# Local attention scores held once per head, their softmax weights copied out over the head elements by transfers, and new orders for the first half

## The chip, the cores and the metric

The kernel runs on one NeuronCore of a Trainium2 chip. Its engines are TensorE (PE), VectorE (DVE), ScalarE (ACT), GpSimd (POOL) and SyncE (SP, which here only issues transfers). Each engine runs its own instructions strictly in order and waits on semaphores for the others. The metric is the device time of one launch in microseconds, median of the runs.

## What is computed

Two layers on x of 8 images of 512 tokens by 128 channels, all in 32-bit floats. Each layer is an attention part and a mixture of experts (8 experts, two per token).

The change lies in layer 0's attention part. A 64-wide projection of the layer-normalised x is split into two branches of 32 channels, with 8 heads of 4 elements each. Branch 0 uses windows of 10 tokens, branch 1 windows of 20, both rolled by half a window:

```python
attn = jnp.einsum('bnqhd,bnkhd->bnhqk', q * scale, k)
attn = attn + bias[None, None]
if amask is not None:
    attn = attn + amask[None, :, None]
attn = jax.nn.softmax(attn, axis=-1)
out = jnp.einsum('bnhqk,bnkhd->bnqhd', attn, v).reshape(Bx, nW, window, C)
```

So every image has 52 windows of 10 and 26 to 28 of 20 tokens, and one small softmax for each window, head and query. Behind it stand an output projection, a residual, an RMS norm and a feed-forward part (GELU), and beside it the experts (a gated unit of 128 units), which every token visits twice, and a shared expert. Layer 1 is a global attention over 512 tokens and another mixture of experts; the change leaves it alone.

## The kernel before, in words

**Stages.** All eight images are first normalised and projected down ("stats", "norm", "down", then "xi", about the first 83 us). Then comes a long software pipeline, layer 0. It ends at about 573 us; layer 1 follows and takes the rest.

**What is in the pipeline.** Two streams are interleaved. One is the chain of images: per image b the steps `("window", b, n)`, `("qk", b, n)`, the pieces "sub1" and "mul1", and `("tail", b, k)`. The other is 31 "passes" k (8 of the shared expert, 23 of blocks of 512 sorted token rows): "sorted" (the rows of the block turned on TensorE), "pair" (up-projections), "gate", "clip", "silu", "act", "down_e" and "yev". GpSimd also sends all token rows to their sorted places in DRAM ("send", 64 indirect transfers); pass 8 and later passes can only load their rows once all were sent.

**What sets the order.** `plan0(engine)` gives each step a due time in slots and sorts by it. An image begins every 9 slots, a pass every 3. The table `MOVED` shifts kinds of steps on one engine by fractions of a slot. So the tables decide the order on every engine, and nothing is reordered at run time.

**Attention of one image, before.** The partitions hold 4 groups of windows by 32 channels (8 heads by 4 elements). Per partition that is 13 windows of 10 by 10 and 7 of 20 by 20, 1300 + 2800 = 4100 elements.
- GpSimd forms q times k for every element (`products`, L1162) in 10 chunks, into `G`.
- TensorE multiplies with `HEADSUM` (L654), a block matrix of 4 by 4 ones: it sums the 4 elements of a head and writes the sum four times, once to each of its partitions. So scores stand four times in PSUM bank 4 or 5.
- VectorE adds bias (and mask) on the way to `WS` (L1430, 10 adds), takes row maxima into `WM` (L1402), subtracts them in branch 0 (L1438); GpSimd subtracts in branch 1 (L1170, 7 pieces). ScalarE takes exponentials of all 4100 elements. VectorE sums them (L1406) and takes reciprocals (L1408).
- The weights times v: branch 0 on VectorE (L1443), branch 1 on GpSimd (L1179, 7 pieces "mul1"). VectorE reduces over keys (L1414) and scales by the reciprocal (L1415) into `WO`, which TensorE projects (L666, L670) in tail step 0.

**Others that the prediction meets.** L1474 is a pass's gate product, L1481 and L1484 its clips. L1137 is a reciprocal root on GpSimd, L1220 the low part of a split of layer 1 weights, L1217 adds a bias. L440 is SyncE's one helper for all its transfers. `passing` loads a pass's weights and rows, `split` stores split weights, "yev" stores an expert block.

## Time and profile before

| | |
|---|---|
| Median of 3 runs | 1521.94 us (1521.86 to 1532.23) |
| Span of the profiled execution | 1519.2 us |
| PE, DVE, ACT, POOL busy | 1045.4, 1030.7, 663.6, 584.1 us |
| Mean granted TensorE clock | 0.840 |
| Until the pipeline's start, the pipeline, the rest | 82.8, 490, 946 us |

The page gives the profiled execution's span, from the first to the last instruction, and no other time for it; it is 2.7 us under the median. The shares of busy time are averages over stages with quite different limits, so the rows below are taken from single stretches.

### The profile page before, as it was taken

The page shows a single profiled execution, that of the slowest core. Times are in us where ns is not written, and L with a number is a line of the kernel's source. Part 1 is how long each engine was busy: PE and PEld are TensorE (multiplying, and loading weights), DVE is VectorE, ACT ScalarE, POOL GpSimd, SP SyncE. Part 2 cuts the span into 40 slices and gives each one's busy share as a digit, 9 for nine tenths or more (in the row PEclk, how much of TensorE's full clock was granted, in tenths as well). Part 3 has the DMA queues.
Part 4 walks back from the last instruction along what each step waited for, and adds up shares of the span by engine and source line. Part 5 has one row for each costly group of instructions (what it writes and reads, how often), then busy time and mean ns, then how long its engine had stood idle before and what let it go on. Part 6 is the DMA issues. An engine that isn't in the chain of part 4 may idle for free.

```text
span 1519.2 us, 16287 instructions
## 1 busy us (share of the span) xinstructions
PE 1045.4 (69%) x5366; PEld 569.4 (37%) x5366; DVE 1030.7 (68%) x1481; ACT 663.6 (44%) x909; POOL 584.1 (38%) x591
## 2 busy tenths in 40 slices
PE   4456365777787680263785757999977878787885
PEld 4423133444444340122232215888832323232331
DVE  3376366998899842378979635666667867686871
...
DMA packets 77948, 126.41 MB, mean 83 GB/s; under 512 B 16297, under 2 KB 35242, under 8 KB 77866
## 3 DMA queue, kind: packets, MB, share of 16 engines
...
q10 hardware_dynamic: 480, 0.79, 0.4%
...
## 4 chain that ended last, share of the span: by engine, by line
PE 33%; DVE 20%; POOL 16%; issue 10%; ACT 8%; DMA 8%; SPq 4%; ACTq 0%; POOLq 0%; DVEq 0%
PE PS L846 6%; PE PS L702 6%; DMA KS<-MAG 4%; POOL XS0D L1204 4%; POOL XS1D L1253 4%; PE PS L865 4%; SPq L440 4%; ACT P L913 4%; DVE MX L1647 3%; PE PS L604 3%; PE PS L609 2%; POOL WS L1179 2%; PE PS L769 2%; PE PS L805 2%; PE PS L823 2%
## 5 line engine op out<-in xcount | busy, mean ns | idle before, releaser
L1647 DVE TENSOR_REDUCE MX<-PS 128x2 f32<-128x1024 f32 x256 | 306.2, 1222 | 128.4 <-PE PS L785 122.6
L913 ACT ACTIVATE P<-PS 128x1024 f32<-128x1024 f32 x256 | 262.3, 1025 | 177.4 <-PE PS L823 174.0
L785 PE MATMUL PS<-KS,QS 62*128 62x512 f32 x512 | 141.9, 552 | 73.4 <-DVE MX L1647 47.6
L1235 POOL DMA_INDIRECT A<-Y1D,POS x64 | 74.3, 1161 | 266.8 <-DMA Y1D<-YE 184.8
L823 PE MATMUL PS<-QS,KS 64*128 64x512 f32 x512 | 125.4, 486 | 68.0 <-ACT P L913 56.6
L805 PE MATMUL PS<-P,V 128*32 128x512 f32 x1024 | 157.3, 691 | 0.1
L785 PEld LDWEIGHTS PS<-KS,QS 62*128 62x128 f32 x512 | 54.3, 209 | 218.5 <-DVE MX L1647 107.5
L702 PE MATMUL PS<-XST,WB 128*128 128x512 f32 x184 | 107.6, 718 | 11.0 <-issue 11.0
L654 PE MATMUL PS<-G,HEADSUM 128*128 128x400 f32 (+2 forms) x160 | 75.2, 592 | 55.4 <-POOL G L1162 44.7
L846 PE MATMUL PS<-XRH,WH 128*128 128x512 f32 (+1 forms) x276 | 104.2, 419 | 0.0
L1261 POOL TENSOR_TENSOR MAG<-MAG,EH 128x1024 f32<-128x1024 f32 x7 | 16.5, 2358 | 225.2 <-ACT MAG L913 225.1
L823 PEld LDWEIGHTS PS<-QS,KS 64*128 64x128 f32 x512 | 54.3, 207 | 117.3 <-ACT P L913 93.8
L1162 POOL TENSOR_TENSOR G<-QKV 128x400 f32<-128x400 f32 (+1 forms) x80 | 73.5, 919 | 37.5 <-ACT QKV L930 29.1
L1235 POOL DMA_INDIRECT YG<-Y0D,POS x64 | 64.7, 1011 | 48.3 <-DMA Y0D<-YE 29.2
L1253 POOL DMA_INDIRECT XS1D<-XN,POS x64 | 64.6, 1010 | 48.3 <-DVE POS L1377 29.1
L1204 POOL DMA_INDIRECT XS0D<-XN,POS x64 | 65.7, 1026 | 27.4 <-issue 23.6
L913 ACT ACTIVATE TH<-PS 128x512 f32<-128x512 f32 (+1 forms) x69 | 41.2, 598 | 76.1 <-PE PS L846 76.0
L865 PEld LDWEIGHTS PS<-W,A 128*128 128x128 f32 (+1 forms) x552 | 71.9, 191 | 6.5
L1170 POOL TENSOR_TENSOR WS<-WS,WM 128x400 f32<-128x400 f32 x56 | 57.8, 1032 | 41.5 <-DVE WM L1402 37.9
L865 PE MATMUL PS<-W,A 128*128 128x128 f32 (+1 forms) x552 | 72.4, 274 | 0.0
L1582 DVE SCALAR_TENSOR_TENSOR SL<-TH,PS 128x512 f32<-128x512 f32 (+1 forms) x69 | 47.2, 683 | 37.1 <-ACT TH L913 37.0
L1179 POOL TENSOR_TENSOR WS<-WS,QKV 128x400 f32<-128x400 f32 x56 | 61.4, 1096 | 20.8 <-DVE WM L1406 17.1
...
## 6 DMA issues: line engine op xcount, KB each, us to landing
...
```

The lines of the kernel that those rows point to most:

```text
L702: ins = pe.matmul(PS[:, 2 * pair + m, :], w[:, at:at + 128], x, start=True, stop=True)
L785: signal(pe.matmul(PS[:, s % 4, :], QS[rows, u % 3, hp, 128 * t:128 * t + 128], KS[rows, u % 3, hp, :], start=True, stop=True), "ms")
L805: ins = pe.matmul(PS[32 * a:32 * a + 32, 6, :], V[:, u // 2 % 2, k, at:at + 32], P[:, m % 2, a, :], start=k == 0, stop=k == NT - 1)
L823: signal(pe.matmul(PS[:, 4 + s % 2, :], KS[rows, u % 3, hp, 128 * k:128 * k + 128], QS[rows, u % 3, hp, :], start=True, stop=True), "st")
L846: ins = pe.matmul(out, WH[:, j % 2, w, f:f + m], x[:, j % 2, :], start=n == 0, stop=n == 2)
L865: ins = pe.matmul(PS[:, 4 + j % 2, 128 * t:128 * t + 128], A4[0:m, q % 3, 128 * t:128 * t + 128], W2[0:m, j % 2, c, :], start=c == 0 and t ...
L913: act.activation(*a, **k).then_inc(sem[name], 1)
L1179: go(f"wpv{r}", pool.tensor_tensor(t, t, bc(v, [128, hi - lo, k, k], 2), ALU.mult))
L1204: pool.indirect_dma_start(XS0D, bass.IndirectOffsetOnAxis(POS[0][:, k, g:g + 1], 0), XN[:, g, :], None).then_inc(sem["sent"], 16)
L1235: pool.indirect_dma_start(dst[:, k, t, :], None, src, bass.IndirectOffsetOnAxis(pos[:, k, g:g + 1], 0)).then_inc(sem[name], 16)
L1253: pool.indirect_dma_start(XS1D, bass.IndirectOffsetOnAxis(POS[1][:, k, g:g + 1], 0), XN[:, g, :], None).then_inc(sem["sent1"], 16)
L1647: go("mx", dve.tensor_reduce(MX[:, u % 2, t].rearrange("p (o h) -> p o h", o=2)[:, :, hp], PS[:, s % 4 - 1:s % 4 + 1, :], AX.X, ALU.max))
```

## The change

**Scores once per head.** `HEADSUM` becomes 128 by 32 with ones for the 4 elements of each head. One matmul gives 32 rows of scores (4 groups of windows by 8 heads) for 400 columns, and four (or three) of them, with different columns of `G`, fill the four blocks of 32 partitions of one PSUM bank. All scores of an image are then 3 groups of 400 per partition, 1200 elements instead of 4100, in the new tile `WD`: groups 0 and 1 are branch 1 (4 and 3 windows), group 2 is branch 0.

**Then, on 1200 elements:** 3 adds of bias and mask on VectorE, 2 maxima, the subtraction of both branches on GpSimd ("less", 2 instructions), one exponential, 2 sums and one reciprocal of 80 on VectorE, and a new multiplication of weights by reciprocal on GpSimd ("even", 2 instructions).

**Weights copied out.** `spread` on SyncE's queue copies them from `WD` to `WS`: 11 transfers an image, each reading 32 partitions four times and writing 128 partitions, 1600 or 1200 bytes to each, in all 2.10 MB (7 of them, 1.43 MB, for branch 1, then 4, 0.67 MB, for branch 0). The products with v are all on GpSimd (branch 0 in 2 pieces, "mul0"), and VectorE's reduction over keys gives `WO` directly. `WS` is single now, `QKV` triple, `G` four rows of 400.

**Orders.** The window steps run over 21 slots instead of 19, the `MOVED` table is new, and SyncE has shifts of its own. TensorE turns a block's rows 3 slots earlier. Before the pipeline, GpSimd builds the bias tables before it waits for the sums of squares, not after; the masks come from DRAM.

```diff
-PIECES = {"sub1": ONES_OF, "mul1": ONES_OF}
...
+GROUPS = 3
+QK_AT = {5: 0, 7: 1, 9: 2}
+PIECES = {"mul0": [(0, 6), (6, 13)], "mul1": [(w, w + 1) for w in range(NWIN[1])]}
+PIECE_AT = {"mul0": 17, "mul1": 17.5}
...
-CHUNK_AT = {5: (0, 2), 6: (2, 4), 7: (4, 6), 8: (6, 8), 9: (8, 10)}
-WEXP_AT = (12, 13)
-FRONT = 19
+LESS_AT, EXP_AT, SUM_AT, EVEN_AT, SPREAD_AT, OUT_AT = 11.5, 12, 13, 13.5, 14, 20
+FRONT = 21
+CELL = WIN[1] ** 2
+TURN0 = 3
...
+MOVED = {'POOL': {('window', 11): 0.1, 'send': -0.9, ('tail', 2): 1.0, ('qk', 6): -0.6, 'sub1': -1, ('qk', 5): -1, 'split': 2.9, 'mul0': 0.6, ('qk', 2): 1.9, ('less', 0): 1.0, 'mul1': -1.1, ('tail', 3): 0.1, ('less', 1): -0.6}, 'DVE': {('tail', 1): 0.7, 'yev': 1.4, ('window', 14): -1.5, ('qk', 9): 1.5, ('window', 18): 0.1, ('qk', 6): 0.4, ('window', 11): 1.0, ('qk', 8): 0.1, ('qk', 7): 0.3, ('window', 20): -0.6, 'clip': 0.1, 'act': 0.4, ('window', 13): 0.6, ('tail', 3): 0.6, ('window', 10): 0.1, ('window', 7): -0.3}, 'PE': {'down_e': 1.7, ('tail', 6): -1, ('window', 10): 1.7, ('tail', 7): -0.8, ('window', 8): 0.8, ('window', 6): 0.7, 'sorted': -3.0, ('tail', 1): -0.6, ('tail', 0): -0.7, ('window', 3): -0.1, ('tail', 4): 0.5, ('pair', 1): 1, ('window', 4): -0.1}, 'ACT': {('tail', 6): -1, ('tail', 2): -0.6, ('window', 3): 0.8, 'split': 1.8, ('tail', 0): -0.7, 'sorted': -2.6, ('window', 4): 0.1, ('window', 12): 0.1, 'silu': 1, ('gate', 0): -0.1}, 'plan': {'period': 9, 'step': 3, 'start': 1}, 'SP': {('window', 14): 2.4, ('pair', 0): 1.9, 'yev': 5.8, 'split': 5.8}}
...
+        for r in (1, 0):
+            put(period * b + LESS_AT, ("less", b, r))
+            put(period * b + EVEN_AT, ("even", b, r))
...
+            QKV = [sb0(f"QKV{r}", [128, 3, 3, GRP[r]]) for r in range(2)]
+            G = sb0("G", [128, 4, CELL])
+            WD = sb0("WD", [128, 2, GROUPS, CELL])
+            WM = sb0("WM", [128, 2, 40])
+            WS = sb0("WS", [128, S_W])
...
+        def window_rows(r, b):
+            return (WD[:, b % 2, 0:2] if r else WD[:, b % 2, 2:3]).rearrange("p c (n k) -> p (c n) k", k=WIN[r])
...
+            def spread(b):
+
+                sp.wait_ge(sem["weven"], 2 * b + 2)
+                for r in (1, 0):
+                    if b:
+                        sp.wait_ge(sem[f"wout{r}"], b)
+                    wide = WS[:, S_AT[r]:S_AT[r] + GRP[r] * WIN[r]].rearrange("p (w a) -> p w a", a=WIN[r] ** 2)
+                    for s in range(4):
+                        rows = slice(32 * s, 32 * s + 32)
+                        if r:
+                            for p in range(2 if s < 3 else 1):
+                                load(wide[:, 4 * p + s], bc(WD[rows, b % 2, p], [32, 4, CELL], 1), "wide1")
+                        else:
+                            n = TURN0 + (s == 3)
+                            src = WD[rows, b % 2, 2, 0:n * WIN[0] ** 2]
+                            dst = wide[:, TURN0 * s:TURN0 * s + n].rearrange("p w a -> p (w a)")
+                            load(dst, bc(src, [32, 4, n * WIN[0] ** 2], 1), "wide0")
+
             for what, *a in plan0("SP"):
...
+                if n - 1 in QK_AT:
+                    c = QK_AT[n - 1]
+                    pe.wait_ge(sem["prod"], GROUPS * b + c + 1)
+                    if c == 2:
+                        pe.wait_ge(sem["S_sb"], GROUPS * b + 1)
+                    else:
+                        pe.wait_ge(sem["qkv_sb"], 2 * b + 2)
+                    flat = G[:].rearrange("p s a -> p (s a)")
+                    for s in range(4 - (c == 1)):
+                        at = TURN0 * WIN[0] ** 2 * s if c == 2 else CELL * s
+                        ins = pe.matmul(PS[32 * s:32 * s + 32, 4 + c % 2, 0:CELL], HEADSUM[:], flat[:, at:at + CELL],
+                                        start=True, stop=True)
+                    signal(ins, "S")
 
...
-                if n in WEXP_AT:
-                    r = WEXP_AT.index(n)
-                    act.wait_ge(sem[f"wsub{r}"], len(PIECES.get(f"sub{r}", "1")) * (b + 1))
-                    s = WS[:, b % 2, S_AT[r]:S_AT[r] + GRP[r] * WIN[r]]
-                    go(f"wexp{r}", s, s, ACT.Exp)
+                if n == EXP_AT:
+                    act.wait_ge(sem["wsub"], 2 * b + 2)
+                    go("wexp", WD[:, b % 2], WD[:, b % 2], ACT.Exp)
...
+            def less_max(r, b):
 
                 pool.wait_ge(sem[f"wmax{r}"], b + 1)
-                k = WIN[r]
-                at = slice(*(x * k for x in piece))
...
+                t = window_rows(r, b)
+                go("wsub", pool.tensor_tensor(t, t, bc(WM[:, r], [128, 40, WIN[r]], 2), ALU.subtract))
+
+            def even(r, b):
+
+                pool.wait_ge(sem["wsum"], b + 1)
+                t = window_rows(r, b)
+                go("weven", pool.tensor_tensor(t, t, bc(WM[:, r], [128, 40, WIN[r]], 2), ALU.mult))
...
-                pool.wait_ge(sem[f"wexp{r}"], b + 1)
-                pool.wait_ge(sem[f"wsum{r}"], b + 1)
+                pool.wait_ge(sem[f"wide{r}"], 16 * (4, 7)[r] * (b + 1))
...
                 elif what == "xi":
-                    pool.wait_ge(sem["xi_sq"], 1)
-                    rsqrt(RSTDX[:], SQX[:], 1.0 / 64, 1e-6, "rstd_xi")
-                    pool.wait_ge(sem["w_b"], 16 * 18)
...
+                    pool.wait_ge(sem["xi_sq"], 1)
+                    rsqrt(RSTDX[:], SQX[:], 1.0 / 64, 1e-6, "rstd_xi")
...
-            def window_sum(b, r):
-                dve.wait_ge(sem[f"wexp{r}"], b + 1)
-                go(f"wsum{r}", dve.tensor_reduce(WM[r][:], window_scores(b, r), AX.X, ALU.add))
-                dve.wait_ge(sem[f"wsum{r}"], b + 1)
-                step(dve.reciprocal(WM[r][:], WM[r][:]))
+                dve.wait_ge(sem["S_sb"], GROUPS * b + (3, 2)[r])
+                if b:
+                    dve.wait_ge(sem["weven"], 2 * b)
+                go(f"wmax{r}", dve.tensor_reduce(WM[:, r], window_rows(r, b), AX.X, ALU.max))
+
+            def window_sum(b):
+                dve.wait_ge(sem["wexp"], b + 1)
+                for r in range(2):
+                    ins = dve.tensor_reduce(WM[:, r], window_rows(r, b), AX.X, ALU.add)
+                step(ins)
+                go("wsum", dve.reciprocal(WM[:], WM[:]))
...
-                step(dve.tensor_reduce(WO[r][:], window_scores(b, r), AX.X, ALU.add))
-                go(f"wout{r}", dve.tensor_tensor(WO[r][:], WO[r][:], WM[r][:], ALU.mult))
+                wide = WS[:, S_AT[r]:S_AT[r] + GRP[r] * WIN[r]].rearrange("p (n k) -> p n k", k=WIN[r])
+                go(f"wout{r}", dve.tensor_reduce(WO[r][:], wide, AX.X, ALU.add))
...
+                if n - 2 in QK_AT:
+                    c = QK_AT[n - 2]
+                    dve.wait_ge(sem["S"], GROUPS * b + c + 1)
+                    if c == 0 and b >= 2:
+                        for r in range(2):
+                            dve.wait_ge(sem[f"wout{r}"], b - 1)
+                    bias = LAST[0] if c == 2 else (BIAS, LAST)[c][1]
+                    flat = "p w q k -> p (w q k)" if c else "p q k -> p (q k)"
+                    rows = 96 if c == 1 else 128
+                    go("S_sb", dve.tensor_tensor(WD[0:rows, b % 2, c], PS[0:rows, 4 + c % 2, 0:CELL],
+                                                 bias[0:rows].rearrange(flat), ALU.add))
+                    dve.wait_ge(sem["S_sb"], GROUPS * b + c + 1)
...
-        "headsum": np.kron(np.eye(32, dtype=np.float32), np.ones((4, 4), np.float32)),
+        "headsum": np.kron(np.eye(32, dtype=np.float32), np.ones((4, 1), np.float32)),
```

Three places of the new orders. The first is GpSimd in the middle of the pipeline, from the last products of an image to the first of its products with v (`wide1` and `wide0` are the semaphores of the copies). Before:

```order
L1162 TENSOR_TENSOR G<-QKV 128x500 [waits S,prod] x2
L1162 TENSOR_TENSOR G<-QKV 128x300 [waits S,prod]
L1220 TENSOR_TENSOR SPL<-STAGE,SPH 128x704 [waits split_hi,prod]
L1170 TENSOR_TENSOR WS<-WS,WM 128x400 [waits wmax1,split_lo]
L1170 TENSOR_TENSOR WS<-WS,WM 128x400 [waits wmax1,wsub1] x6
L1136 TENSOR_SCALAR VAR<-SQ 128x4 [waits sqs0,wsub1]
L1137 TENSOR_TENSOR SCALES<-VAR,NHALF 128x4 [waits pstep]
L1162 TENSOR_TENSOR G<-QKV 128x400 [waits qkv_sb,rstd0]
...
L1217 TENSOR_TENSOR X<-X,FB 128x512 [waits h0,prod]
...
L1179 TENSOR_TENSOR WS<-WS,QKV 128x400 [waits wsum1,wexp1,prod]
L1179 TENSOR_TENSOR WS<-WS,QKV 128x400 [waits wsum1,wexp1,wpv1] x3
```

Now:

```order
L1185 TENSOR_TENSOR G<-QKV 128x700 [waits S,wpv1]
L1185 TENSOR_TENSOR G<-QKV 128x600
L1192 TENSOR_TENSOR WD<-WD,WM 128x800 [waits wmax1,prod]
L1248 TENSOR_TENSOR SPL<-STAGE,SPH 128x704 [waits split_hi,wsub]
L1192 TENSOR_TENSOR WD<-WD,WM 128x400 [waits wmax0,split_lo]
L1198 TENSOR_TENSOR WD<-WD,WM 128x800 [waits wsum,wsub]
L1198 TENSOR_TENSOR WD<-WD,WM 128x400 [waits wsum,weven]
L1185 TENSOR_TENSOR G<-QKV 128x400 [waits S,qkv_sb,weven]
...
L1164 TENSOR_SCALAR VAR<-SQ 128x4 [waits sqs0,prod]
...
L1185 TENSOR_TENSOR G<-QKV 128x400 x2
...
L1205 TENSOR_TENSOR WS<-WS,QKV 128x400 [waits wide1,x1_b]
L1205 TENSOR_TENSOR WS<-WS,QKV 128x400 [waits wide1,wpv1] x3
```

The seven subtractions became two, two multiplications (L1198) stand behind them, with nothing between the second subtraction and the first multiplication, which waits for the sums; and the products with v wait for transfers rather than for VectorE.

The second is VectorE about the softmax of an image; between the rows stand parts of the passes. Before, from the clips of a pass to the sum of branch 1:

```order
L1481 TENSOR_SCALAR UL<-UL 128x512 [waits gused]
L1484 TENSOR_SCALAR UL<-UL 128x512 [waits lused]
...
L1430 TENSOR_TENSOR WS<-PS,LAST 128x300 [waits S,S_sb]
L1402 TENSOR_REDUCE WM<-WS 128x130 [waits S_sb]
L1438 TENSOR_TENSOR WS<-WS,WM 128x1300 [waits wmax0]
...
L1406 TENSOR_REDUCE WM<-WS 128x130 [waits wexp0]
L1408 RECIPROCAL WM<-WM 128x130 [waits wsum0]
L1443 TENSOR_TENSOR WS<-WS,QKV 128x1300 [waits step]
L1414 TENSOR_REDUCE WO<-WS 128x130 [waits aux_full,wpv0]
...
L1406 TENSOR_REDUCE WM<-WS 128x140 [waits wexp1]
```

Now, from the last reduction of an image over keys (L1444) to the reciprocal of the next image (L1437):

```order
L1444 TENSOR_REDUCE WO<-WS 128x140 [waits wpv1]
L1484 TENSOR_TENSOR XN<-PS,X 128x512 [waits x1_b,aux_full]
L1494 SCALAR_TENSOR_TENSOR UL<-PS,WB,H 128x512 [waits aux_free,a,h3g,gpair]
...
L1504 TENSOR_SCALAR UL<-UL 128x512 [waits lused]
L1456 TENSOR_TENSOR WD<-PS,LAST 128x400 [waits S]
L1430 TENSOR_REDUCE WM<-WD 128x40 [waits weven,S_sb]
L1524 SCALAR_TENSOR_TENSOR YE<-B,PS 128x512 [waits sto1,y]
L1511 SCALAR_TENSOR_TENSOR AA<-UL 128x512 [waits y,lc,th]
L1435 TENSOR_REDUCE WM<-WD 128x40 [waits wexp]
...
L1437 RECIPROCAL WM<-WM 128x80 [waits step]
```

Rows with 1300 and 2800 inputs are gone save for L1444; the reduction of branch 1 of one image comes ahead of the last scores (L1456, L1430) of the next.

The third is SyncE, which now issues the copies (L447, WS<-WD) between a pass's loads and an expert block's store:

```order
L447 DMA STAGE<-in_w 128x352 x2
...
L447 DMA WB<-in_wb 128x644
...
L447 DMA XS<-XS0D 128x512 [waits aux_full]
L447 DMA WS<-WD 128x1x400 [waits wout1,weven]
L447 DMA WS<-WD 128x1x400 x6
L447 DMA WS<-WD 128x1x300 [waits wout0]
L447 DMA WS<-WD 128x1x300 x2
L447 DMA WS<-WD 128x1x400
L447 DMA Y0D<-YE 128x512 [waits yev]
L498 TENSOR_LOAD EB [waits yev]
```

Before, no such copies stood there; the store waited for `yev` right behind the loads, and the weight loads for `y` instead of `yev`.

## Rows read from the trace of the kernel before

**Rows 1.** The cores: span, and mean granted clock of TensorE.
```profile
core 0: 1519.2 us, clock 0.840
```

**Rows 2.** Three stretches: length, busy time (instructions) by engine, PEclk, DMA share, GB/s.
```profile
109.50:234.00 124.50, 61.77 (x252) 32.32 (x252) 66.47 (x76) 24.43 (x42) 103.48 (x103) 0.73 0.16 55
293.00:475.00 182.00, 141.03 (x736) 81.23 (x736) 164.05 (x174) 93.45 (x157) 118.59 (x113) 0.89 0.28 85
506.00:573.00 67.00, 50.89 (x204) 29.27 (x204) 41.21 (x55) 32.32 (x54) 13.97 (x14) 0.86 0.21 67
```

**Rows 3.** VectorE by line, 293 to 475 us: count, busy us, mean ns, idle before.
```profile
L1406 DVE TENSOR_REDUCE WM<-WS 128x140 f32<-128x2800 f32 (+1 forms) x9 | 21.3, 2365 | 0.0
...
L1430 DVE TENSOR_TENSOR WS<-PS,BIAS 128x400 f32<-128x400 f32 (+1 forms) x32 | 19.1, 596 | 3.8 <-PE PS L654 3.0
...
L1402 DVE TENSOR_REDUCE WM<-WS 128x140 f32<-128x2800 f32 (+1 forms) x8 | 18.3, 2288 | 0.3
...
L1414 DVE TENSOR_REDUCE WO<-WS 128x140 f32<-128x2800 f32 (+1 forms) x8 | 18.3, 2282 | 0.1
...
L1474 DVE SCALAR_TENSOR_TENSOR UL<-PS,WB,H 128x512 f32<-128x512 f32 x24 | 17.6, 748 | 10.9 <-ACT H L913 6.4 <-issue 4.3
...
L1484 DVE TENSOR_SCALAR UL<-UL 128x512 f32<-128x512 f32 x13 | 14.1, 1084 | 0.0
...
L1481 DVE TENSOR_SCALAR UL<-UL 128x512 f32<-128x512 f32 x12 | 10.3, 855 | 0.0
...
L1408 DVE RECIPROCAL WM<-WM 128x140 f32<-128x140 f32 (+1 forms) x8 | 8.0, 997 | 0.3
...
L1438 DVE TENSOR_TENSOR WS<-WS,WM 128x1300 f32<-128x1300 f32 x4 | 6.1, 1513 | 0.1
```

**Rows 4.** GpSimd by line, the same stretch.
```profile
L1162 POOL TENSOR_TENSOR G<-QKV 128x400 f32<-128x400 f32 (+2 forms) x41 | 37.7, 921 | 14.7 <-ACT QKV L930 10.3 <-PE PS L654 1.7
L1179 POOL TENSOR_TENSOR WS<-WS,QKV 128x400 f32<-128x400 f32 x28 | 31.0, 1106 | 10.6 <-DVE WM L1406 8.7
L1170 POOL TENSOR_TENSOR WS<-WS,WM 128x400 f32<-128x400 f32 x28 | 30.1, 1074 | 22.7 <-DVE WM L1402 20.8
L1137 POOL TENSOR_TENSOR SCALES<-VAR,NHALF 128x4 f32<-128x4 f32 x4 | 7.8, 1942 | 0.3
L1220 POOL TENSOR_TENSOR SPL<-STAGE,SPH 128x704 fp32r<-128x704 f32 x4 | 6.7, 1676 | 0.3
L1217 POOL TENSOR_TENSOR X<-X,FB 128x512 f32<-128x512 f32 x4 | 5.1, 1269 | 0.3
```

**Rows 5.** ScalarE by line, the same stretch: the exponential.
```profile
L913 ACT ACTIVATE WS<-WS 128x1300 f32<-128x1300 f32 (+1 forms) x8 | 15.3, 1910 | 13.0 <-DVE WS L1438 13.0
```

**Rows 6.** GpSimd by line, 109 to 235 us.
```profile
L1204 POOL DMA_INDIRECT XS0D<-XN,POS x64 | 65.7, 1026 | 27.4 <-issue 23.6 <-POOL WS L1170 1.4 <-POOL G L1162 1.4
```

**Rows 7.** Subtraction of the maxima by tile, whole run: count, ns min/median/max, first and last start.
```profile
L1170 POOL TENSOR_TENSOR WS<-WS,WM x56: 863/866/2217, 143.0 to 505.1; 128x400 f32<-128x400 f32 x56
```

**Rows 8.** TensorE in order of time: start us, us, line, count.
```profile
353.21 1.75 PE L654 MATMUL PS<-G,HEADSUM 128*128 128x400 f32 x4 [0.79 <-DVE WS L1430]
...
422.89 1.52 PE PS L641 x48
```

**Rows 9.** Stretches in which all DMA engines are busy, columns as in rows 2.
```profile
1404.00:1412.00 8.00, 7.08 (x52) 2.98 (x50) 5.77 (x5) 5.83 (x8) 2.65 (x3) 1.00 1.09 137
20.00:40.00 20.00, 12.57 (x59) 12.06 (x57) 6.77 (x34) 1.79 (x3) 2.49 (x4) 1.00 1.04 371
```

**Rows 10.** SyncE's issues of layer 1's copies inside SBUF: count, ns min/median/max.
```profile
L440 SPq DMA_DIRECT2D QS<-EH x64: 551/608/1235, 632.3 to 1430.9; - x64
```

**Rows 11.** Before the pipeline, in order of time: GpSimd, then VectorE.
```profile
74.22 3.50 POOL L1193 COPY BIAS<-RPB 128x10 f32<-128x10 f32 x10
...
81.63 1.03 POOL L1196 TENSOR_TENSOR LAST<-LAST,BIAS 128x400 f32<-128x400 f32 x1
...
82.69 0.42 DVE L1319 TENSOR_REDUCE RS<-PS 128x32 f32<-128x256 f32 x1 [6.21 <-POOL LAST L1196]
```

153 lines of the change are left out of this document (57 added, 96 removed), and 2 rows, old and new, of the table SIGNALS.

## The prediction, made before the changed kernel had run

> **What bounds the kernel now.** The core's row [rows 1] gives one span, 1519.2 us, 2.7 us under the median of the runs, so every sum below is made against 1519.2 and 2.7 is added at its end. I then read busy time by stretch [rows 2], because the change touches the first 573 us alone.
>
> From 109.5 to 234 us GpSimd is the bound: 103.5 of 124.5 us busy, and the 64 sends alone are 65.7 us with 23.6 us of issue gaps between them [rows 6]. Busy and gaps together fill the stretch. From 234 to 506 us lie six image periods, 272 / 6 = 45.4 us each. In four of them (293 to 475 us, 182 / 4 = 45.5) VectorE is busy 164.05 us, 41.0 an image or 90%; GpSimd 118.6, 29.6 an image; TensorE 141 [rows 2]. GpSimd idles ahead of its subtractions because of VectorE's maxima (20.8 us) and ahead of its values products because of VectorE's sums (8.7) [rows 4], and ScalarE ahead of the exponentials likewise (13.0) [rows 5]. So VectorE sets the period. From 506 to 573 us no engine is full: the last image and the last passes follow each other.
>
> **Rates per element**, each from a row: VectorE's reduction 2288 / 2050 = 1.12 ns [rows 3]; on GpSimd q times k 921 / 410 = 2.25, weights times v 1106 / 400 = 2.77 [rows 4], subtraction at its median 866 / 400 = 2.17 [rows 7]; ScalarE's exponential 1910 / 2050 = 0.93 [rows 5].
>
> **VectorE, per image** [rows 3]. Bias adds: 10 inputs of some 0.58 (5.8 us) become 3 (1.7): -4.1. Maxima 4.6 to 1200 x 1.12 = 1.35: -3.2. Sums the same: -3.2. Reciprocals 2.0 to 0.6 (80 columns in place of 270): -1.4. L1438, branch 0's subtraction, 1.5, goes to GpSimd, and so does its equal, branch 0's product with v: -3.0. The reduction over keys (L1414) stays at 4.6; its scaling goes, at a price I leave out. Together about -15, leaving some 26 of 41. VectorE is no longer the bound.
>
> **TensorE, per image.** HEADSUM takes 10 matmuls of up to 128 x 500 now; four records, two to a matmul, last 1.75 us [rows 8], so 0.88 a matmul and some 9 us. If the four blocks of 32 columns run beside each other, it is three times 0.88 = 2.6 us. The trace has matmuls into four such blocks: 24 of them, of 130 or 140 columns, in 1.52 us [rows 8]. One after the other at the HEADSUM's rate they would be 24 x 0.88 x 135 / 400 = 7.1. So I take 2.6. Were it otherwise, 11 x 0.88 = 9.7: TensorE has 182 - 141 = 41 us idle in four images and bears a microsecond more; only the loop below would feel part of it.
>
> **GpSimd, per image.** Products 9.2 as before. Subtractions: 7 pieces, 7.5 us, become 1200 x 2.25 = 2.7. "Even" is new: 2.7. Values: 2800 + 1300 elements x 2.77 = 11.3 instead of 7.8. Reciprocal root, split, and bias (L1137, L1220, L1217) 1.9 + 1.7 + 1.3. Together 30.8, where it is 29.6 now. So no engine's busy time fills 45 us any more; what counts is the loop through the single `WS`: values products, reduction over keys, the next copies, the next values products.
>
> **The loop, from the end of an image's last product with v (t = 0)**, in the order the engines have. VectorE: reduction of 2800 elements 3.1; then a residual add 0.75 (priced as the gate product of the same size), two gate products 1.5, two clips 1.9 [rows 3], the last bias add 0.6, maximum of 400 elements 0.45, that is 8.3. GpSimd's subtraction of 400 elements: 9.2. ScalarE's exponential of 1200: 10.3. VectorE's sums and reciprocal, 1.35 + 0.6, and handovers: 12.6. GpSimd, with nothing to do from 9.2 to 12.6, then "even": 15.3. Now it forks.
> - GpSimd: the products of 2800 elements 6.3, reciprocal root 1.9, bias of x 1.3 and gaps: about 25.0.
> - Transfers: 1.43 MB for branch 1, then 0.67 MB for branch 0. The trace of before has no copy of this form. **Bounds:** the slowest stretch with all DMA engines full is of layer 1's copies inside SBUF, 137 GB/s; the fastest, a zero fill from SBUF, 371 [rows 9]. I take 137, since it is the one of copies from SBUF to SBUF. With an estimated 1.5 us for start and receipt: branch 1 lands at 15.3 + 1.5 + 10.5 = 27.3, branch 0 at 32.2. Issuing seven copies at 0.61 each [rows 10] is 4.3 and hidden.
>
> From 27.3 GpSimd makes branch 1's pieces, 7.8, with then branch 0's, 3.6 (landed at 32.2, so no more waiting): 38.7, and with 1.3 for handovers and gaps **40 us a period**. At 371 it would be 25.0 + 11.4 + 0.6 = 37, since then GpSimd is later than the transfers. A period of 45.4 again would need branch 0 to land at 45.4 - 1.3 - 3.6 = 40.5, that is 2.10 MB in 23.7 us, 89 GB/s.
>
> First what the rows show: 137 GB/s with the engines full. The Trainium skill, "SBUF — State Buffer", section "Door 1: The DMA port swizzle", speaks against the change: partitions 0 to 31 reach 8 of the 16 ports, half the rate, and 0 to 63 no more than these. Each copy reads 32 partitions. Half of the zero fill's 371 by that rule is 186, with which branch 1 lands at 24.5 and branch 0 at 28.1, so the period would be 37; half of 137 gives the slow rival below. The copies of layer 1 read 64 partitions each, and by that page have their halving behind them; no run here shows which.
>
> **What else the change adds to.** SyncE waits for "even" in the middle of its queue; behind the wait stand the store of an expert block (its tile is double, so a pass of some 13 us covers it) and the next pass's weights. Other traffic is 85 GB/s over the period [rows 2], 3.9 MB an image, 1.3 MB a pass; I have it beside the copies at no cost, see the third rival. ScalarE loses 2 x 1.9 - 1.1 = 2.7 us an image of exponentials, worth nothing by itself.
>
> **The sum.**
> - Start: VectorE waited 6.21 us for `LAST`, since the tables (first copy at 74.22) stood on GpSimd behind the reciprocal root [rows 11]. Now they are made before that wait: -6.2.
> - Sends, 109.5 to 234: still GpSimd. Counted in both orders, what stands between first and last send is 34 us in the new one and some 35 in the old one at the same rates: -2, ends 0 and -4.
> - Steady: 6 x (45.4 - 40) = -32.
> - 506 to 573: the last passes have VectorE for themselves sooner and their rows are turned earlier, but an image takes 21 slots instead of 19: -4, ends 0 and -10.
> Together -44.2: 1519.2 - 44.2 + 2.7 = **1477.7, say 1477 us**. Its own range 1462 to 1490. Chance 0.47.
>
> **Rivals.**
> - *Copies quick*: at 165 GB/s or more, GpSimd's own work is the later branch; period 37, -18: 1459. For it: 371 and the page's rule on the wider figure. 0.20.
> - *Copies behind a pass's loads*: SyncE issues the weights and rows of a pass right ahead of them. 1.3 MB at 371 GB/s is 3.5 us, all of it on the loop: period 43.5, +21: 1498. Against it: `weven` comes long after these issues as a rule. 0.22.
> - *VectorE's wait only changed place*: the work of the passes between the steps of the softmax (VectorE, in order, waits for ScalarE's gates 6.4 us in four images [rows 3]) draws the loop out to today's 45.4: -12: 1510. 0.07.
> - *Slower*: reading 32 partitions four times over halves 137 to 68 GB/s. Branch 0 lands at 15.3 + 1.5 + 30.9 = 47.7, its product, handovers and gaps make a period of 52.6, 6 x 7.2 = +43 against before, less the 12.2 of the other terms: 1553. It decides where the period passes 45.4 + 12.2 / 6 = 47.4, which is 82 GB/s. Against it: the copies that gave 137 write only 16 partitions each and so are narrower than these, which write all 128. 0.04.
>
> Under 1% (15 us) I can't tell from no change. Cases below 1506.7: the forecast, the first two rivals and a small part of the third: **0.90**; within 1%: 0.06; slower: 0.04. The range takes in the quick copies and those behind loads: **1450 to 1506**.
>
> **What would show it.** In the trace after: VectorE busy near 26 us an image; HEADSUM's four matmuls in 0.8 us; the wait ahead of GpSimd's first product with v named as the copies, and of 2 us; a gap of 3 us ahead of "even" named as VectorE's reciprocal; copies 9 to 11 us from the first issue to branch 1's landing; the pipeline's end at about 573 - 44 = 529 us. No wait for the copies, and GpSimd busy through, would be the first rival; a late wait on SyncE's queue or a landing 14 us after "even" the second. The prediction is wrong in its foundation if the period is set elsewhere than on GpSimd and the copies, for instance by TensorE (35 us an image busy now, about 30 then), which at a low granted clock (0.73 in the stage of the sends [rows 2]) would come close to 40.

## The result: 1471.9 us, 3.4% less

The median is 1471.93 us (1468.32 to 1473.38, 4 runs) against 1521.9 before; the ratio is 0.9656 with a 95% interval of 0.9625 to 0.9686. The prediction was 1477. In the profile the span is 1470.1 us against 1519.2 [rows 1], 49.1 less. The number is close, but the copies, on which I had built the 40 us period, did not set it.

Two marks cut layer 0 in both traces: the first and last send, and the first gather of expert rows (YG), which ends the pipeline. Rows by tile of the kernel before, with first and last start:

```profile
L1204 POOL DMA_INDIRECT XS0D<-XN,POS x64: 957/962/2165, 109.5 to 232.1; - x64
L1235 POOL DMA_INDIRECT YG<-Y0D,POS x64: 943/955/1742, 576.2 to 752.2; - x64
```

And of the changed kernel:

```profile
L1230 POOL DMA_INDIRECT XS0D<-XN,POS x64: 955/962/1300, 106.3 to 220.0; - x64
L1263 POOL DMA_INDIRECT YG<-Y0D,POS x64: 943/955/1745, 525.5 to 700.8; - x64
```

So 3.2 us are won by the first send, 8.9 between first and last send (122.6 to 113.7), 38.6 from there to the first gather (344.1 to 305.5), and 1.6 are lost behind (943.0 to 944.6). That is 49.1.

The same views as [rows 2] to [rows 4], over four periods of the changed kernel (from one image's first product with v to that of the fourth image after it) and over the sends; first the stretches:

```profile
289.20:442.40 153.20, 122.98 (x747) 71.51 (x744) 96.08 (x124) 82.67 (x153) 116.40 (x104) 0.87 0.58 156
106.30:221.00 114.70, 39.34 (x188) 20.23 (x186) 37.30 (x53) 20.30 (x31) 94.75 (x92) 0.65 0.23 67
```

VectorE is busy 24.0 us an image (41.0 before, 26 expected), TensorE 30.7, GpSimd 29.1 of some 38. GpSimd by line in the four periods:

```profile
L1205 POOL TENSOR_TENSOR WS<-WS,QKV 128x400 f32<-128x400 f32 (+2 forms) x36 | 43.2, 1200 | 3.0 <-DMA WS<-WD 0.2
L1185 POOL TENSOR_TENSOR G<-QKV 128x400 f32<-128x400 f32 (+2 forms) x36 | 37.1, 1059 | 8.9 <-PE PS L683 5.7 <-issue 1.8 <-POOL WD L1198 0.9
L1192 POOL TENSOR_TENSOR WD<-WD,WM 128x800 f32<-128x800 f32 (+1 forms) x8 | 9.7, 1209 | 9.2 <-DVE WM L1430 8.9
L1198 POOL TENSOR_TENSOR WD<-WD,WM 128x800 f32<-128x800 f32 (+1 forms) x8 | 9.7, 1209 | 14.6 <-DVE WM L1437 14.3
```

The right-hand numbers are the thing to read: they are GpSimd's idle time ahead of a line's instructions and what ended it. Ahead of the products with v (L1205) GpSimd waits 0.2 us in four images for the copies. Its idle time lies elsewhere: 3.6 us an image ahead of "even" for VectorE's reciprocal (3.4 expected), 2.2 for the maximum, 1.4 for TensorE's scores. One period in order of time:

```profile
327.82 11.48 POOL L1205 TENSOR_TENSOR WS<-WS,QKV 128x400 f32<-128x400 f32 x9
339.37 2.56 POOL L1185 TENSOR_TENSOR G<-QKV 128x700 f32<-128x700 f32 x2
342.01 1.54 POOL L1192 TENSOR_TENSOR WD<-WD,WM 128x800 f32<-128x800 f32 x1
343.63 1.68 POOL L1248 TENSOR_TENSOR SPL<-STAGE,SPH 128x704 fp32r<-128x704 f32 x1
347.85 0.87 POOL L1192 TENSOR_TENSOR WD<-WD,WM 128x400 f32<-128x400 f32 x1 [2.54 <-DVE WM L1430]
352.29 2.50 POOL L1198 TENSOR_TENSOR WD<-WD,WM 128x800 f32<-128x800 f32 x2 [3.56 <-DVE WM L1437]
```

SyncE issues the 11 copies right behind "even" of the image before, from 315.41 on (GpSimd had ended it at 315.39):

```profile
315.41 9.71 SPq L447 DMA_DIRECT2D WS<-WD  x11
```

That is 0.88 us an issue on average and 4.1 us (the median) from an issue to its landing, so branch 1 is complete 6 x 0.88 + 4.1 = 9.4 us after the first issue by these two; a wait in a later run (even_dve_qkv, below) gives 10.1. So it is there at some 325 to 325.5, and the product that needs it starts at 327.82: two microseconds or more to spare. The period, from the first products at 289.17 to those at 478.77, is 189.6 / 5 = 37.9 us.

The five periods are not alike. The first four, in the columns of [rows 2]:

```profile
289.17:327.82 38.65, 31.43 (x186) 18.46 (x186) 23.31 (x31) 20.39 (x38) 28.99 (x27) 0.82 0.63 168
327.82:365.61 37.79, 30.73 (x189) 17.77 (x189) 24.32 (x31) 20.58 (x39) 29.13 (x27) 0.86 0.53 147
365.61:405.77 40.16, 32.48 (x189) 18.95 (x189) 24.38 (x31) 20.93 (x39) 29.14 (x27) 0.83 0.63 169
405.77:442.44 36.67, 28.41 (x192) 16.33 (x189) 24.11 (x31) 20.84 (x40) 29.16 (x27) 0.95 0.51 137
```

GpSimd's work is the same in each, 29.0 to 29.2 us. The shortest period is the one with TensorE's highest granted clock, 0.95, the two longest those with 0.82 and 0.83 (1.00 is 2.4 GHz, and these are means of stretches at 2.4 and at 1.2). In the period of 40.16 GpSimd waits 2.53 us for TensorE's scores, in that of 36.67 not at all. So GpSimd's chain runs through TensorE too, and the period goes with its clock. Which of the two leads isn't shown, since no run changes the clock alone. The fifth period (36.33) has no next image's products to make, and 2.41 us of waiting for the copies.

### The profile page after: what moved, and what is told of

Same layout as the page of the kernel before. It is cut to its first block, busy times and chain, and to the rows that moved or that the text cites. A ratio compares the mean times of both kernels' runs of the same rounds, so it can differ in the third digit from the quotient of the medians.

```text
span 1470.1 us, 16140 instructions
## 1 busy us (share of the span) xinstructions
PE 1004.3 (68%) x5382; PEld 548.7 (37%) x5382; DVE 900.9 (61%) x1385; ACT 645.6 (44%) x902; POOL 578.9 (39%) x570
## 4 chain that ended last, share of the span: by engine, by line
PE 23%; DVE 11%; DMA 7%; ACT 7%; POOL 6%; issue 5%; SPq 4%; ACTq 0%; DVEq 0%; POOLq 0%
PE PS L876 6%; DMA KS<-MAG 4%; POOL XS1D L1281 4%; PE PS L895 4%; ACT P L943 4%; SPq L447 4%; DVE MX L1667 3%; PE PS L835 3%; PE PS L853 2%; PE PS L799 2%; PE PS L815 2%; ACT MAG L943 1%; PE PS L637 1%; DVE MAG L1596 1%; PE PS L632 1%
## 5 line engine op out<-in xcount | busy, mean ns | idle before, releaser
L815 PE MATMUL PS<-KS,QS 62*128 62x512 f32 x512 | 143.1, 557 | 70.1 <-DVE MX L1667 40.1
L732 PE MATMUL PS<-XST,WB 128*128 128x512 f32 x184 | 100.1, 686 | 0.0
L1185 POOL TENSOR_TENSOR G<-QKV 128x400 f32<-128x400 f32 (+2 forms) x72 | 73.5, 1048 | 41.0 <-ACT QKV L960 15.4
L1205 POOL TENSOR_TENSOR WS<-WS,QKV 128x400 f32<-128x400 f32 (+2 forms) x72 | 85.3, 1184 | 8.0 <-DMA WS<-WD 2.6
L1281 POOL DMA_INDIRECT XS1D<-XN,POS x64 | 64.0, 1000 | 48.3 <-DVE POS L1405 29.1
L1263 POOL DMA_INDIRECT YG<-Y0D,POS x64 | 64.3, 1005 | 37.6 <-DMA Y0D<-YE 18.5
L1230 POOL DMA_INDIRECT XS0D<-XN,POS x64 | 62.9, 983 | 24.7 <-issue 21.4
L1494 DVE SCALAR_TENSOR_TENSOR UL<-PS,WB,H 128x512 f32<-128x512 f32 x46 | 34.0, 748 | 57.0 <-ACT H L943 43.4
```

The costliest lines, as they stand in the source:

```text
L732: ins = pe.matmul(PS[:, 2 * pair + m, :], w[:, at:at + 128], x, start=True, stop=True)
L815: signal(pe.matmul(PS[:, s % 4, :], QS[rows, u % 3, hp, 128 * t:128 * t + 128], KS[rows, u % 3, hp, :], start=True, stop=True), "ms")
L1185: ins = pool.tensor_tensor(dst, bc(q[:, lo:hi], full, 3), bc(kk[:, lo:hi], full, 2), ALU.mult)
L1205: go(f"wpv{r}", pool.tensor_tensor(t, t, bc(v, [128, hi - lo, k, k], 2), ALU.mult))
L1263: pool.indirect_dma_start(dst[:, k, t, :], None, src, bass.IndirectOffsetOnAxis(pos[:, k, g:g + 1], 0)).then_inc(sem[name], 16)
L1281: pool.indirect_dma_start(XS1D, bass.IndirectOffsetOnAxis(POS[1][:, k, g:g + 1], 0), XN[:, g, :], None).then_inc(sem["sent1"], 16)
```

## Experiments

The kernels ran on three chips: start_back, the copies twice and few, and even_later on one, after_again, even_dve, even_dve_qkv and headsum_full on the second, the rest on the third. On the first and third the kernel before took 1592 and 1590 us, on the second 1522. The difference lies in layer 1: from the first gather to the end it is 1012.8 us in start_back and 944.6 in the changed kernel, while the first send of every kernel but start_back lies between 105 and 107 us. So each kernel is read by the start of its first gather, the end of layer 0's pipeline: 525.5 us in the changed kernel, 576.2 before. Ratios are to the kernel before on the same chip. On the first and third chip there is no trace of the changed kernel or of the one before; that layer 0 takes the same time there isn't shown directly. But what each run saves against the kernel before by full times on its own chip (57.0 us for copies_few, say) agrees within 5 us with what its first gather says (56.0), in every run.

### The start

GpSimd's tables again behind the sums of squares (start_back):

```diff
                 elif what == "xi":
+                    pool.wait_ge(sem["xi_sq"], 1)
+                    rsqrt(RSTDX[:], SQX[:], 1.0 / 64, 1e-6, "rstd_xi")
                     pool.wait_ge(sem["w_b"], 16 * 20)
...
-                    pool.wait_ge(sem["xi_sq"], 1)
-                    rsqrt(RSTDX[:], SQX[:], 1.0 / 64, 1e-6, "rstd_xi")
```

> The changed kernel with one thing undone: GpSimd again builds the bias tables behind its wait for the sums of squares and the reciprocal root. Theory: VectorE's routing reductions start at 82.7 us again instead of 77.1, the first send moves from 106.3 back to about 109.5, and the kernel takes 3 to 6 us more, 1475 to 1478. Rival: the sends start when the routing is done, which other work sets, and the start was worth nothing: 1472.

Ratio 0.9752 (0.9701 to 0.9803). VectorE's wait is back:

```profile
82.94 0.42 DVE L1347 TENSOR_REDUCE RS<-PS 128x32 f32<-128x256 f32 x1 [6.41 <-POOL LAST L1222]
```

The first send is at 110.8 (106.3), the first gather at 529.7: 4.2 us. VectorE's routing starts 5.8 us later than in the changed kernel (82.94 against 77.11), the first send only 4.5; what takes up the rest isn't shown. So a wait of 6.2 us was worth 4.2.

### The copies: twice, few, half

Seven more transfers an image, ahead of branch 1's, to a scratch area (copies_twice):

```diff
-                                load(wide[:, 4 * p + s], bc(WD[rows, b % 2, p], [32, 4, CELL], 1), "wide1")
+                                for dst in (WXD[4 * p + s], wide[:, 4 * p + s]):
+                                    load(dst, bc(WD[rows, b % 2, p], [32, 4, CELL], 1), "wide1")
...
-                pool.wait_ge(sem[f"wide{r}"], 16 * (4, 7)[r] * (b + 1))
+                pool.wait_ge(sem[f"wide{r}"], 16 * (4, 14)[r] * (b + 1))
```

> Seven more transfers an image, each of the same source and size as one of branch 1's copies and issued ahead of it, to a scratch area of DRAM that nobody reads; GpSimd waits for all. Theory (GpSimd's own chain sets the 38 us, the copies are limited by SyncE's 0.88 us an issue and come 2 us before they are needed): branch 1 is 7 x 0.88 = 6.2 us later, 4 us a period, six or seven times: about 1472 + 27 = 1499. Rival (the DMA engines move copies at 137 GB/s and set the period): 1.43 MB more are 10.5 us a period, 1472 + 65 = 1537 or more.

Ratio 0.9888 (0.9833 to 0.9942), first gather 555.4: +29.9 where the theory had +27 and the rival +65. Now the copies are waited for, 4.2 us in each of five images:

```profile
L1207 POOL TENSOR_TENSOR WS<-WS,QKV 128x400 f32<-128x400 f32 (+2 forms) x45 | 52.3, 1163 | 24.0 <-DMA WS<-WD 20.8
```

Three copies an image in place of eleven, from the second image on (copies_few):

```diff
-                            for p in range(2 if s < 3 else 1):
+                            for p in range((2 if s < 3 else 1) if not b else int(s == 0)):
...
-                        else:
+                        elif s == 0 or not b:
...
-                pool.wait_ge(sem[f"wide{r}"], 16 * (4, 7)[r] * (b + 1))
+                pool.wait_ge(sem[f"wide{r}"], 16 * ((4, 7)[r] + b))
```

> The computation is changed: from the second image on only the first two copies of branch 1 and the first of branch 0 are made, so most partitions multiply stale weights. 3 transfers an image instead of 11. Theory (copies are covered by GpSimd's chain): no more than the 2.4 us of the last image, 1469 to 1472. Rival (copies on the path at 137 GB/s): 10 us a period less, 1472 - 50 = 1420.

Ratio 0.9647 (0.96 to 0.9693), first gather 520.2, 5.3 us less, of which the theory explains the last image's 2.4. The first four periods are 37.6 us each, where they average 38.3 in the changed kernel; the fifth, with its wait for the copies gone, is 32.9 for 36.3. Part of that comes back behind it. By this the copies are covered in all images but the last: eight fewer bought 0.7 us in each of four periods, where the rival had 10. And even the 0.7 need not be theirs, since TensorE's clock was higher too (0.91 against 0.87).

Half the columns in each copy, 200 of 400, or 200 of 300 and 400 (copies_half):

```diff
-                                load(wide[:, 4 * p + s], bc(WD[rows, b % 2, p], [32, 4, CELL], 1), "wide1")
+                                h = CELL // 2 if b else CELL
+                                load(wide[:, 4 * p + s, 0:h], bc(WD[rows, b % 2, p, 0:h], [32, 4, h], 1), "wide1")
...
-                            n = TURN0 + (s == 3)
+                            n = (TURN0 + (s == 3)) if not b else 2
```

> The computation is changed: from the second image on each of the 11 copies moves half of its columns (200 of 400, or 200 of 300 and 400), the rest stays stale. Theory (the DMA engines limit the train of copies: 200 KB per 0.88 us is 233 GB/s, and SyncE's issue takes 0.55 us when nothing holds it): the train of 11 issues shortens from 9.5 to about 6.5 us and a copy's landing from 4.1 to about 3.5 us. Rival (SyncE's issue of such a transfer takes 0.88 us by itself): the train stays at 9.5 us. In both, layer 0's pipeline ends within 5 us under 525, as with copies_few (520).

There is a single run of this, so no ratio. The train of issues is shorter:

```profile
313.48 7.09 SPq L447 DMA_DIRECT2D WS<-WD  x11
```

7.09 / 11 = 0.64 us an issue, near the 0.608 of [rows 10], against 0.88: the full-width train was held back by the transfers themselves, at 2.10 MB in 9.7 us, 216 GB/s. That is the pace of the issues; from 319 to 329 us, while the copies land, the DMA engines of the changed kernel move 213 GB/s in all, at a busy share of 0.91:

```profile
319.00:329.00 10.00, 10.00 (x51) 5.30 (x50) 6.27 (x11) 6.47 (x9) 7.62 (x9) 1.00 0.91 213
```

The landing fell from 4.1 to 3.6 us. The first gather came at 514.2, sooner than with copies_few and 6 us under what was expected; the period was 36.1 (286.77 to 467.26, five of them; 37.9 in the changed kernel). Part of it is seen in the waits: over five images GpSimd waited 1.3 us for TensorE's scores where it was 5.7 in the changed kernel, at a granted clock of 0.92 against 0.86 (289 to 440 us). Why the clock was higher there, and so how much of the 11 us belongs to the copies, stays open.

### Filling GpSimd's gap

The next image's first products ahead of "even", into its 3.56 us (even_later):

```diff
-'mul0': 0.6, ('qk', 2): 1.9
+'mul0': 0.6, ('even', 0): 0.6, ('even', 1): 0.6, ('qk', 2): 1.9
```

> Only the order on GpSimd is changed: the products of the next image's first chunk (4 x 400, 3.3 us) come ahead of the two multiplications by the reciprocal, into the 3.56 us in which GpSimd waits for VectorE's sums and reciprocal. Theory (GpSimd's chain sets the period): 3.3 us leave the chain, but the copies had only 2 us to spare, so the period falls by about 2 us and GpSimd then waits some 1.3 us for branch 1's copies: 1472 - 13 = 1459. Rival (another engine or the copies set the 38 us): no change or slower, 1472 to 1480.

Ratio 0.9867 (0.9805 to 0.9929), first gather 548.5: 23 us **more**. The theory, that GpSimd's own chain is the whole story, fell. GpSimd, then ScalarE's copy of q, k and v:

```profile
355.79 0.88 POOL L1192 TENSOR_TENSOR WD<-WD,WM 128x400 f32<-128x400 f32 x1 [1.90 <-DVE WM L1430]
364.77 3.32 POOL L1185 TENSOR_TENSOR G<-QKV 128x400 f32<-128x400 f32 x4 [8.10 <-issue]
368.17 2.50 POOL L1198 TENSOR_TENSOR WD<-WD,WM 128x800 f32<-128x800 f32 x2
```

```profile
362.12 0.89 ACT L960 ACTIVATE QKV<-PS,QKVB 128x130 f32<-128x130 f32 x3 [3.01 <-PE PS L669]
363.44 0.91 ACT L960 ACTIVATE QKV<-PS,QKVB 128x140 f32<-128x140 f32 x3 [0.43 <-PE PS L669]
```

The products can't fill the gap: their inputs aren't there until ScalarE's last copy of q, k and v ends at 364.35. "even", moved behind them, was held up with them, and so were the copies (17.8 us of waiting in five images) and SyncE's queue. In the changed kernel the same copy of q, k and v ended at 354.3 and "even" at 354.8, so the one hid the other:

```profile
352.61 1.69 ACT L960 ACTIVATE QKV<-PS,QKVB 128x130 f32<-128x130 f32 x6 [1.43 <-PE PS L669]
```

### Is it that, or GpSimd's chain?

The changed kernel once more, beside the next three (after_again):

> The changed kernel as it is, on the chip of the runs beside it, to compare them with. The first gather of expert rows (the end of layer 0's pipeline) stands at 525 us again, within 1 us.

1471.29 us, ratio 0.9673 (0.9653 to 0.9693), first gather 525.5 again, although the single periods differ from those above (37.6, 40.1, 36.6, 38.6 and 37.5 us).

"even" on VectorE, behind its reciprocal (even_dve):

```diff
                 go("wsum", dve.reciprocal(WM[:], WM[:]))
+                dve.wait_ge(sem["wsum"], b + 1)
+                for r in (1, 0):
+                    t = window_rows(r, b)
+                    go("weven", dve.tensor_tensor(t, t, bc(WM[:, r], [128, 40, WIN[r]], 2), ALU.mult))
...
                 elif what == "even":
-                    even(a[1], a[0])
+                    pass
```

> The two multiplications by the reciprocal are made by VectorE, right behind its reciprocal, not by GpSimd: 2.5 us of work and 3.56 us of waiting leave GpSimd's chain in each period of 38. Theory A (GpSimd's chain alone sets the period): 6 us a period less, the pipeline's end at 525 - 36 = 489 us, unless the copies take over: 1 us earlier by themselves, so then -2 to -3 a period, 510. Theory B (the next image's q, k and v come from ScalarE at the same time, at 354.3 against 352.3 for the reciprocal, and GpSimd's next products wait for them): at most 0.5 to 1 us a period, the end at 519 to 523.

1464.41 us, ratio 0.9622 (0.9596 to 0.9648), first gather 516.6. GpSimd has lost 2.5 us of work and the 3.56 us wait, and has a new one in their place:

```profile
343.33 0.87 POOL L1192 TENSOR_TENSOR WD<-WD,WM 128x400 f32<-128x400 f32 x1 [2.35 <-DVE WM L1430]
350.01 3.32 POOL L1185 TENSOR_TENSOR G<-QKV 128x400 f32<-128x400 f32 x4 [5.81 <-issue]
```

```profile
348.09 1.79 ACT L960 ACTIVATE QKV<-PS,QKVB 128x130 f32<-128x130 f32 x6 [1.44 <-PE PS L669]
```

It starts 0.13 us after the copy of q, k and v ended (349.88). The period is 37.0 (284.95 to 470.06, five of them) against 37.9: 0.9 us, as theory B had it, though the end lies 2.4 us below B's range; theory A's 489 or 510 us is ruled out. It is the fastest version on this chip, with the next one level with it.

The same, with q, k and v sooner (even_dve_qkv):

```diff
-('window', 3): 0.8, ('window', 4): 0.1
+('window', 3): 0.05, ('window', 4): 0.1
...
-('pair', 1): 1, ('window', 4): -0.1}
+('pair', 1): 1, ('window', 4): -0.8}
```

> As even_dve, and two shifts in the orders: ScalarE copies the turned tokens (XIT) ahead of the exponential instead of behind it and behind a pass's rows, and TensorE makes q, k and v ahead of the up-projection of the attention output. Theory B: q, k and v are there 2 us earlier, so 2.5 us a period go: the end at 525 - 17 = 508 us. Theory A: the same as even_dve.

1465.13 us, ratio 0.963 (0.9599 to 0.9662), first gather 519.1: no gain, a miss for theory B's number. ScalarE shows one price of the new place:

```profile
342.91 0.68 ACT L951 ACTIVATE XIT<-PS,N1W 64x512 f32<-64x512 f32 x1 [0.93 <-PE PS L637]
343.50 0.25 ACT L943 ACTIVATE XIT<-PS,N1W 64x10 f32<-64x10 f32 x1
343.77 1.28 ACT L943 ACT_TABLE_LOAD   x1
345.06 1.20 ACT L943 ACTIVATE WD<-WD 128x1200 f32<-128x1200 f32 x1
```

GpSimd's subtraction was done at 343.80, the exponential starts at 345.06. In even_dve the table load lay in the idle time before (at 342.06) and the exponential started 0.04 us after the subtraction. Counted from the end of that subtraction, q, k and v are there 1.15 us sooner than in even_dve (4.53 us for 5.68), and the exponential starts 1.2 us later.

There is a second price, of about the same size. GpSimd's next products now start in the same moment as VectorE's two multiplications by the reciprocal, and both take longer. VectorE, then GpSimd:

```profile
348.48 2.84 DVE L1441 TENSOR_TENSOR WD<-WD,WM 128x800 f32<-128x800 f32 x2
```

```profile
348.46 4.40 POOL L1185 TENSOR_TENSOR G<-QKV 128x400 f32<-128x400 f32 x4 [4.66 <-issue]
```

In even_dve, where VectorE is done (349.14) before GpSimd begins (350.01), the same instructions take 1.48 and 3.32 us. It is so in all four images behind which a next one follows; in the fifth, where GpSimd has no products to make, VectorE's two multiplications are back at 1.48 us. Both prices together put the first copy 2.6 us later behind the subtraction (7.55 us for 4.96), and GpSimd now waits for the copies:

```profile
361.43 1.03 POOL L1205 TENSOR_TENSOR WS<-WS,QKV 128x400 f32<-128x400 f32 x1 [0.77 <-DMA WS<-WD]
```

This wait also gives the landing time directly: the first issue was at 351.35, so branch 1's last copy had landed 10.1 us later.

### TensorE's column blocks

The four matmuls of a group made 128 wide and summed into one bank, same result (headsum_full):

```diff
-            HEADSUM = sb0("HEADSUM", [128, 32])
+            HEADSUM = sb0("HEADSUM", [128, 224])
...
-                        ins = pe.matmul(PS[32 * s:32 * s + 32, 4 + c % 2, 0:CELL], HEADSUM[:], flat[:, at:at + CELL],
-                                        start=True, stop=True)
+                        ins = pe.matmul(PS[:, 4 + c % 2, 0:CELL], HEADSUM[:, 96 - 32 * s:224 - 32 * s],
+                                        flat[:, at:at + CELL], start=s == 0, stop=s == 3 - (c == 1))
```

> The four matmuls of a group of scores are 128 columns wide and add up in one PSUM bank (a zero-padded HEADSUM shifted by 32 columns each time), so they can't run beside each other; the result is the same. Theory (the column blocks do run side by side, 8 records in 0.88 us): a group takes 3.5 us instead of 0.9, 7 us a period more on TensorE, and two of the three groups are waited for in GpSimd's chain, so 3 to 5 us a period: layer 0's pipeline ends at 525 + 20 to 32 = 545 to 557 us. Rival (TensorE's score matmuls have slack): within 3 us of 525.

1499.99 us, ratio 0.9879 (0.9818 to 0.994), first gather 553.0. A group in this kernel, then in the changed one:

```profile
330.28 2.85 PE L683 MATMUL PS<-G,HEADSUM 128*128 128x400 f32 x8
```

```profile
321.93 0.88 PE L683 MATMUL PS<-G,HEADSUM 128*32 128x400 f32 x8
```

That is 2.0 us more a group, both at a granted clock of 1.00. The group that TensorE makes at a low clock, behind a wait, takes 4.65 us in this kernel (353.85, at 0.63) and 1.55 in the changed one (344.84, at 0.57), 3.1 more. The period is 4.2 us longer (296.33 to 506.66, five of 42.1). GpSimd's waits show where: over five images 15.6 us for TensorE's scores where it was 5.7, and 25.6 us for VectorE's maximum, which follows the last group, where it was 10.9, so 2.0 and 2.9 us a period. Two of the three groups lie on the loop. With the sums made in this way, and not side by side, the change would have kept 23 of its 51 us in layer 0.

### One more move to VectorE

even_dve, with branch 0's product with v on VectorE too (even_mul0_dve), and then with the two shifts of even_dve_qkv as well (even_mul0_dve_qkv):

```diff
-PIECES = {"mul0": [(0, 6), (6, 13)], "mul1": [(w, w + 1) for w in range(NWIN[1])]}
+PIECES = {"mul0": [(0, 13)], "mul1": [(w, w + 1) for w in range(NWIN[1])]}
...
             def window_out(b, r):
+                if r == 0:
+                    dve.wait_ge(sem["wide0"], 16 * 4 * (b + 1))
+                    t = WS[:, 0:1300].rearrange("p (w q k) -> p w q k", w=13, q=10)
+                    v = QKV[0][:, b % 3, 2, :].rearrange("p (w k) -> p w k", k=10)
+                    go("wpv0", dve.tensor_tensor(t, t, bc(v, [128, 13, 10, 10], 2), ALU.mult))
```

> As even_dve, and branch 0's product with v (1300 elements, 3.6 us on GpSimd) on VectorE in one instruction of 1.5 us, as it was before the change. Theory: GpSimd's values products and with them everything behind them in the loop (products, subtraction) come 3.6 us sooner; VectorE adds 1.5 us there, in an idle gap: the period falls from 37.5 to about 34.5, the pipeline's end from 516.6 to about 497, the time to 1445. Rival (the copies land just in time now, and the q, k, v chain through TensorE and ScalarE doesn't get shorter): 1 us a period, 510, 1458.

> As even_mul0_dve, with the two shifts of even_dve_qkv (q, k and v 1.5 us earlier). There they gained nothing, because the copies then came 0.8 us late. Theory: the same here, within 3 us of even_mul0_dve. Rival (with values products shorter, q, k and v decide again): 1 us a period better than even_mul0_dve.

Ratios 0.966 (0.9622 to 0.9697) and 0.9603 (0.957 to 0.9636), first gathers 519.3 and 515.9. The first theory fell (497 us). VectorE in even_mul0_dve, from its wait for ScalarE to the reduction of branch 1, then GpSimd beside it:

```profile
329.09 1.06 DVE L1522 SCALAR_TENSOR_TENSOR AA<-UL 128x512 f32<-128x512 f32 x1 [2.50 <-ACT UL L943]
330.07 2.34 DVE L1450 TENSOR_TENSOR WS<-WS,QKV 128x1300 f32<-128x1300 f32 x1
332.45 1.51 DVE L1455 TENSOR_REDUCE WO<-WS 128x130 f32<-128x1300 f32 x1
333.87 0.97 DVE L1432 TENSOR_REDUCE WM<-WD 128x40 f32<-128x800 f32 x1
334.76 3.06 DVE L1455 TENSOR_REDUCE WO<-WS 128x140 f32<-128x2800 f32 x1
```

```profile
322.68 8.37 POOL L1205 TENSOR_TENSOR WS<-WS,QKV 128x400 f32<-128x400 f32 x7
331.12 3.71 POOL L1185 TENSOR_TENSOR G<-QKV 128x700 f32<-128x700 f32 x2
343.28 0.88 POOL L1192 TENSOR_TENSOR WD<-WD,WM 128x400 f32<-128x400 f32 x1 [5.00 <-DVE WM L1432]
```

GpSimd is done with branch 1 at 331.05, 8.4 us after its start in place of 11.4, but VectorE can't reduce it before 334.76: its product stands in front. From GpSimd's first product to its last subtraction it is 20.6 us, 19.8 in even_dve (323.53 to 343.33). The 1300-element product of VectorE took 2.34 us where it took 1.51 in the kernel before, and GpSimd's two products beside it 3.71 where they take 2.56: the two engines were in each other's way here too. The two shifts, of no use without this move, brought 3.4 us with it. That lies between the theory (within 3) and the rival (1 us a period), and the intervals of the two ratios overlap, so neither is shown.

## The prediction, step by step

- **Start, -6.2.** The wait went, but the first send came only 3.2 us sooner, and undoing it cost 4.2. Right in kind, a third too large or more.
- **Sends, -2, ends 0 and -4.** Measured -8.9. This step failed, and by counting: I had 35 and 34 us of other work between the sends, the trace has 36.8 before and 31.8 now. I had taken 9 rows of subtractions for 9 instructions, and not seen that fewer products fall between the sends. The parts: four subtractions of 4.9 us where 13 pieces took 11.6, 11 product pieces of 10.9 where 16 took 14.7, against 3.0 more of products with v and 2.4 of "even". The sends themselves went from 65.7 [rows 6] to 62.9 us, and all idle time of GpSimd in between from 21.0 to 20.0. The 23.6 us of "gaps between them" that I read from [rows 6] was a misreading; 8.64 of them lie ahead of the first send:

```profile
109.50 1.22 POOL L1204 DMA_INDIRECT XS0D<-XN,POS  x1 [8.64 <-issue]
```

- **Steady, six periods of 40.** Five periods run at 37.9, not 40, against 45.2 between the same marks before: about -37. But the third image's last subtraction starts 52.3 us behind the last send (272.33 against 220.0) and 46.8 before, so 5.5 are given back while the pipeline fills. Sum -31 for an expected -32: two errors that cancel, so the size of this term is luck.
- **Tail, -4, ends 0 and -10.** From the last subtraction to the first gather 71.1 us before, 63.5 now: -7.6. Behind the first gather 1.6 us are lost, for which I had no term. All in all -3.2, -8.9, -31, -7.6 and +1.6 make the 49.1 us; the excess of the start against the shortfall of the sends and the tail is luck as well.
- **The mechanism of the 40** is the step that was wrong: "I take 137". From the end of an image's last product with v (339.30 in the period shown) "even" ended after 15.5 us, where the loop had 15.3, so the chain through VectorE and ScalarE was right. But the copies ran at 216 GB/s and branch 1 landed some 10.1 us behind "even" where I had 12.0, and GpSimd's own branch came to the products with v after 26.3 us (365.61) where I had 25.0. So the later branch was GpSimd's, by a microsecond or two. The 1.5 us for start and receipt in that sum is shown by no run; what the runs show is 4.1 us from a copy's issue to its landing in the train, and 3.6 with half the columns.
- The period was what the rival "copies quick" gave, 37, with its premise, GpSimd later than the transfers; copies_few and copies_twice show it. I had given that rival 0.20. Its sign "GpSimd busy through" did not come: it works 29.1 of 38 us. What its branch missed are the 1.4 us of waiting for TensorE's scores, which come and go with the granted clock, and that q, k and v are ready only when "even" ends.
- The nearest row in kind (layer 1's copies) was a poor neighbour: they write 16 partitions each. The rule of the Trainium skill that I set beside it ("SBUF — State Buffer", "Door 1: The DMA port swizzle": 32 partitions reach half the ports) gave 186 GB/s from the zero fill's 371 [rows 9]; measured were 216. That no further halving comes on top of 137 is thereby shown for this form. The 216 belongs to a train whose transfers read four different blocks of 32 partitions; no run here times copies from one block alone.
- **VectorE** 26 an image: 24.0. **TensorE** 2.6 for the scores: twice 0.88 and once 1.55, at a granted clock of 0.57. **GpSimd** 30.8: 29.1; half of the difference is the reciprocal root, 1.0 us now where [rows 4] had 1.9.
- Of the other rivals, *behind a pass's loads* was not seen: the copies are issued 0.02 us after "even". *Slower* needed under 82 GB/s. *VectorE's wait only changed place* holds in small: 3.6 + 2.2 us an image of GpSimd's idle time are waits for VectorE's softmax steps, but they don't reach 45 us.
